# Adjacency products cut into quarter rows and spread anew over the turns of a two-step graph kernel

## The chip, the core and the metric

The program runs on one core of a Trainium2 chip. The metric is device time in microseconds (us); the median of three runs of the kernel before is 3864.36 us (3864.08 to 3867.04). TensorE (PE) multiplies matrices, VectorE (DVE), ScalarE (ACT) and GpSimd (POOL) work elementwise, and SyncE (SP) issues every DMA here. The engines run side by side, each in its own program order, and meet at semaphores.

## The reference

Two layers over 4096 nodes of 256 features. Layer 0 is graph attention with four heads. Layer 1 is run in two steps; in short:

```python
R = S + eye(N);  R = R / R.sum(-1)          # S is the 0/1 adjacency, 4096 x 4096
for n in range(2):
    A  = top_p_attention(Xa, W1, W2, W3)     # softmax(q @ k.T), kept up to 0.9 of the mass, 4096 x 4096
    Xf = R @ Xf
    Xa = A @ Xa
    Z  = Z + Xf @ U1[n].T + Xa @ U2[n].T
return layernorm(layernorm(X + Z) ... )      # the residual and norm around the layer
```

The change lies in the second of the two attention steps. There the kernel computes, beside the second A, both products with R (the two hops): R @ Xf and R @ (R @ Xf).

## The kernel before, in words

Rows are cut into 32 tiles of 128 nodes. The program is layer 0 (until about 1400 us), the first attention step (`s == 0`, until about 2180 us) and the second one (`s == 1`, to the end). In the second step a loop of *turns* n = 0, 1, 2, ... runs on every engine, with tiles staggered in it.

What TensorE does in turn n, in this order (lines 1056 to 1083): it transposes the finished probabilities of tile n-1 (`Tr`, L1029, 32 transposes), multiplies out the logits of tile n+2 (L984), does a small transpose (`zx`, L993), the product A @ Xa of tile n-1 (`AV`, L1044), a small product (`mq`, L1007), and then adjacency products: `Rmul` is one row tile of R @ Xf, 32 products with 257 columns (L967), whose four quarters use one 512 KB block of the adjacency each. Between two of these rows stands `gather_level` (L1050), one tiny product that brings 128 flags of tile n onto one partition.

A product in f32 is recorded as two MATMULs, so a row of 32 products is 64 records in the trace, and 32 in a listing of the program. There are 64 such rows: 0 to 31 are the first hop, 32 to 63 the second. `pairs_in(n)` says which pair of rows stands in turn n: rows 0 and 1 stand ahead of the turns, rows 2 and 3 in turn 0, rows 2n+2 and 2n+3 in every turn n up to 30.

What VectorE does for tile n: three passes of a threshold search over 128x4096 scores (L1577), one pass for the rest sum (L1583), maxima, a sort of 48 values, `threshold`, whose last instruction (L1637) releases `gather_level(n)` on TensorE. Then `finish(n)`: two marking passes (L1645, L1646), the read of TensorE's flags (L1691), the row maximum of tile n+2 (L1536), and the mask pass over tile n (L1710). The mask pass releases `Tr` of tile n, which is the first work of TensorE in turn n+1.

ScalarE copies results out of PSUM, runs the first three levels of the search for tile n+1 (`level`, L1314 and L1315), the exponentials (L1295), and copies out finished adjacency rows (`r_ev`, L1344). GpSimd computes the bracket for the search (`bracket`, L623 to L642; its L631 releases ScalarE's L1313) and finishes adjacency rows (`r_post`, L670 to L678). Finished rows go out through SP (`rstore`). Adjacency rows and AV share two PSUM banks in turn (`rslot`), and a bank is free once ScalarE has copied it out (`rv`).

SP loads adjacency blocks three ahead (`adjchunk`, a ring of AJR = 3 buffers): the block q+3 is asked for when TensorE is done with block q.

Of the kernel before, what the change touches and what calls it, by code (L numbers as in the profile page):

```python
# [9 lines left out]
ALU = mybir.AluOpType  # L10
# [16 lines left out]
def gat_topp_kernel(nc, xT, x, adj, adjTb, Wp, WT, aT, res_w, bias, res_b, ident, sel,  # L27
# [15 lines left out]
    AJR = 3  # L43
# [4 lines left out]
    RLEAD = 1  # L48
# [3 lines left out]
    fslot = {min(max(HT + m - RLEAD + 2, 2 * m + 4), NT + 1): m for m in range(HT)}  # L52
    LAST = max(fslot)
    DR = NT - 4

    def pairs_in(n):
        if n < 0:
            return [0]
        if n == 0:
            return list(range(1, RLEAD + 1))  # L60
        return [n + RLEAD] if n + RLEAD < NT else []

    ctx = ExitStack()
    with ctx:
# [273 lines left out]
        for s in range(2):  # L338
            g = {}
            names = ("kk", "pl", "el", "mx", "xp", "mask", "av", "rv", "pz", "po", "xs", "acc", "nz", "lv")  # L340
            if s == 0:
                names += ("kq", "ks", "gx", "gd", "lr", "xc")
            else:
                names += ("R", "rd", "hi", "gi", "yd", "ys", "fi", "fa", "s1", "f1", "s2", "fo", "fd", "lt", "e8", "bt",
                          "bf", "tp", "ls", "lp", "lz", "lo")
# [3 lines left out]
            g["xd"] = [sem(f"xd{i}_{s}") for i in range(2)]  # L349
            g["qd"] = [sem(f"qd{i}_{s}") for i in range(2)]  # L350
# [6 lines left out]
        def _(sp):  # L357
# [144 lines left out]
            def adjpairs(n, half):  # L502
                for p in pairs_in(n):
                    for q in range((2 * p + half) * NCH, (2 * p + half + 1) * NCH):
                        adjchunk(q + AJR)

            def rstore(n):
                for p in pairs_in(n):
                    for i in range(2):
                        r = 2 * p + i  # L510
                        sp.wait_ge(g["yd"], r + 1)
                        ld(tile_of(y_d if r < NT else z_d, r % NT), yr[:, i, :], g["ys"])
                    gxload(p + 1)
# [9 lines left out]
            adjpairs(-1, 1)  # L523
            for n in range(LAST + 4):
# [16 lines left out]
                if n in fslot:  # L541
# [10 lines left out]
                    sp.wait_ge(g["ys"], 16 * (NT + 2 * m + 2))  # L552
# [21 lines left out]
        def _(po):  # L574
# [36 lines left out]
            for s in range(2):  # L611
# [54 lines left out]
                def r_post(p):  # L666
                    for i in range(2):
                        r = 2 * p + i
                        po.wait_ge(g["rd"], r + 1)
# [1164 lines left out]
```

## Time and profile before

| | |
|---|---|
| median of three runs | 3864.36 us |
| the profiled execution's own time | 3867.65 us |
| span of its instructions on the core | 3865.9 us |
| mean granted TensorE clock | 0.983 |
| busy: PE, DVE, ACT, POOL | 94%, 92%, 79%, 39% |
| adjacency products (L967) in all | 909.5 us busy, 4096 records |

A timeline row reads: start in us, duration in us, engine, line, operation, out<-in, count; in square brackets, where the engine stood idle before it, how long and what ended the idle time. A row of windows reads: the stretch, its length, busy time (count) of each engine, the granted TensorE clock (1.00 is full speed), the DMA share and GB/s.

### The profile page before, as it was taken

The numbers are of one execution on the slowest core, as the hardware profiler recorded it, in microseconds if no ns is written. First come the engines' busy times: TensorE is split into PE (matmuls) and PEld (weight loads), VectorE is DVE, ScalarE is ACT, GpSimd is POOL, SyncE is SP. The second block draws the span as 40 slices with busy tenths as digits, with TensorE's granted clock in tenths as the row PEclk, the third lists the DMA queues.
The fourth block names the chain that finished last, engine by engine and source line by source line (L and its number), as shares of the span: only waits on it lengthen the run. The fifth ranks groups of instructions, "written<-read, shape, count | busy, mean of one in ns | idle before, by whom it ended". The sixth has DMA issues, their size and how long they took to land.

```text
span 3865.9 us, 66246 instructions
## 1 busy us (share of the span) xinstructions
PE 3617.3 (94%) x25368; PEld 3045.1 (79%) x25368; DVE 3559.9 (92%) x6051; ACT 3063.1 (79%) x3107; POOL 1522.2 (39%) x1627
## 2 busy tenths in 40 slices
PE   8888889889889879999999989999999999999997
PEld 5777778778778758777777768888888888888885
DVE  4999999999999989999999499999999999999998
ACT  6999999999999965555555378888888888888873
POOL 0112111111211210111111156555555569999997
PEclk9999999999999989999999989999999999999998
DMA  3211211211211140000000323333334433333332
GB/s 108 76 57 57 84 58 57 81 61 57 78 64 57 63 135 16 18 17 18 21 18 19 118 78 93 100 97 103 105 105 122 128 107 111 114 113 116 114 119 70
DMA packets 155582, 302.72 MB, mean 78 GB/s; under 512 B 16634, under 2 KB 116986, under 8 KB 151010
## 3 DMA queue, kind: packets, MB, share of 16 engines
q1 hardware_dynamic: 155234, 298.22, 24.2%
q8 instruction: 201, 3.29, 0.4%
q14 instruction: 147, 1.20, 0.1%
HBM read 256.54 MB, written 41.62 MB: 77 GB/s over the span
## 4 chain that ended last, share of the span: by engine, by line
ACT 35%; POOL 22%; DVE 21%; issue 12%; PE 10%; DVEq 0%; DMA 0%; ACTq 0%; SPq 0%; POOLq 0%
ACT b L1122 6%; ACT b L1314 6%; ACT b L1315 6%; ACT b L1135 5%; DVE b L1488 5%; ACT b L1115 4%; DVE b L1710 3%; POOL b L629 3%; POOL b L626 3%; DVE b L1470 3%; DVE b L1598 3%; DVE b L1596 2%; ACT b L1295 2%; POOL b L623 2%; PE ps L882 2%
## 5 line engine op out<-in xcount | busy, mean ns | idle before, releaser
L967 PE MATMUL ps<-b 128*128 128x257 f32 x4096 | 909.5, 382 | 6.2 <-DMA b<-in_adjTb 6.2
L1044 PE MATMUL ps<-b 128*128 128x257 f32 x4096 | 903.7, 380 | 0.0
L967 PEld LDWEIGHTS ps<-b 128*128 128x128 f32 x4096 | 776.4, 190 | 130.7 <-issue 9.7
L1044 PEld LDWEIGHTS ps<-b 128*128 128x128 f32 x4096 | 773.2, 190 | 112.9 <-ACT b L1252 0.8
L882 PE MATMUL ps<-cb,b 128*128 128x128 f32 x4096 | 517.6, 282 | 154.0 <-ACT b L1122 126.3
L882 PEld LDWEIGHTS ps<-cb,b 128*128 128x128 f32 x4096 | 462.3, 145 | 205.8 <-ACT b L1122 141.7
L1470 DVE SCALAR_TENSOR_TENSOR b<-b 128x4096 f32<-128x4096 f32 x128 | 566.5, 4425 | 13.6 <-ACT b L1115 9.3
L1472 DVE CUSTOM_DVE_ANT_0 b<-b 128x4096 f32<-128x4096 f32 x128 | 566.4, 4425 | 4.4
L589 POOL TENSOR_SCALAR b<-b 128x1 f32<-128x1 f32 x128 | 74.7, 584 | 1087.8 <-DVE b L1472 1087.8
L1135 ACT ACTIVATE b<-ps 128x1024 f32<-128x1024 f32 x510 | 487.1, 1051 | 18.2 <-PE ps L882 16.1
L822 PE MATMUL ps<-b 128*64 128x128 f32 x8192 | 488.9, 275 | 0.0
L1122 ACT ACTIVATE b<-b 128x4096 f32<-128x4096 f32 x127 | 476.1, 3749 | 15.6 <-POOL b L589 15.4
L822 PEld LDWEIGHTS ps<-b 128*64 128x64 f32 x8192 | 443.3, 137 | 26.8 <-ACT b L1135 10.9
L1577 DVE SCALAR_TENSOR_TENSOR b<-b 128x4096 f32<-128x4096 f32 x99 | 446.8, 4513 | 3.5
L1314 ACT ACTIVATE b<-b 128x4096 fp8e4<-128x4096 f32 x93 | 345.0, 3710 | 7.9 <-ACT b L1266 5.7
L1315 ACT ACTIVATE b<-b 128x4096 fp8e4<-128x4096 f32 x93 | 345.0, 3709 | 3.0
L1710 DVE SCALAR_TENSOR_TENSOR b<-b 128x4096 f32<-128x4096 f32 (+1 forms) x67 | 287.8, 4299 | 42.7 <-issue 27.4
L1115 ACT ACTIVATE b<-b 128x2560 f32<-128x2560 f32 x128 | 315.8, 2467 | 0.0
L1387 ACT ACTIVATE b<-ps 128x1024 f32<-128x1024 f32 x256 | 242.2, 1031 | 44.5 <-PE ps L1029 44.4
L1029 PE MATMUL ps<-cb,b 128*128 128x128 f32 x2048 | 242.1, 278 | 34.9 <-DVE b L1710 34.0
L1029 PEld LDWEIGHTS ps<-cb,b 128*128 128x128 f32 x2048 | 231.9, 144 | 45.2 <-DVE b L1710 40.6
L1295 ACT ACTIVATE b<-b 128x4096 f32<-128x4096 f32 x64 | 237.0, 3703 | 28.0 <-DVE b L1540 22.7
(212 smaller groups left out, 5038.6 us busy)
## 6 DMA issues: line engine op xcount, KB each, us to landing
b<-in_adjTb SPq DMA_DIRECT2D x256, 512.0 KB, 3.8
b<-in_adj SPq DMA_DIRECT2D x32, 2048.0 KB, 8.3
h_d<-b SPq DMA_DIRECT2D x63, 128.0 KB, 1.8
b<-h_d SPq DMA_DIRECT2D x63, 128.0 KB, 2.6
b<-in_xT SPq DMA_DIRECT2D x4, 1024.0 KB, 9.6
b<-in_xT SPq DMA_DIRECT2D x32, 128.0 KB, 8.1
X_d<-b SPq DMA_DIRECT2D x32, 128.0 KB, 8.3
gx_d<-b SPq DMA_DIRECT2D x32, 128.0 KB, 1.8
```

The lines of the kernel that those rows point to most:

```text
L822: last = mm(bank(6 + t % 2)[half, 128 * h:128 * h + 128], h_s[:, j, 64 * h:64 * h + 64], pt[:, gq % PTR, b, :], start=(j < 2), stop=(j >= ...
L882: last = nc.tensor.transpose(o[:, b * 128:(b + 1) * 128], ub[:, u % UB, j * 128:(j + 1) * 128], ident_s)
L967: last = mm(b[:, 0:XA], aj[:, q % AJR, e, :], xf[:, j, :], start=(j == 0), stop=(j == NT - 1))
L1029: last = nc.tensor.transpose(o[:, b * 128:(b + 1) * 128], scores(s, t)[:, j * 128:(j + 1) * 128], ident_s)
L1044: last = mm(o[:, 0:XA], at[:, q % ATR, b, :], xa[:, j, :], start=(j == 0), stop=(j == NT - 1))
L1115: act(ub[:, u % UB, LSP:N], sd_s[:, h, LSP:N], ACT.Identity, bias=ssc[:, t, h:h + 1]).then_inc(s_e, 1)
L1122: act(b, b, ACT.Exp, bias=nm[:, u % 4:u % 4 + 1], accum_out=zp[:, u % 16:u % 16 + 1]).then_inc(s_x, 1)
L1135: act(pt[:, gq % PTR].rearrange("p a b -> p (a b)"), bank(2 * (i % 3), 2)[:, 0:CW], ACT.Copy).then_inc(s_ev, 1)
L1314: alink(act(junk, e, ACT.Sign, bias=neg, accum_out=C, saturate=False))
L1315: alink(act(junk, e, ACT.Relu, bias=neg, accum_out=S, saturate=False))
L1470: link(v.scalar_tensor_tensor(out=b, in0=b, scalar=SLOPE, in1=b, op0=ALU.mult, op1=ALU.max))
L1472: v.tensor_tensor_reduce(out=b, in0=b, in1=adj_s[t % 2], scale=1.0, scalar=-3.0e38, op0=ALU.mult, op1=ALU.max, accum_out=nm[:, u % 4:u % 4 ...
```

## The change

The plan of adjacency rows is written in quarters (one 512 KB block each, 8 products, 16 records). Rows 0 and 1 still stand ahead of the turns. Turn 0 now holds rows 2, 3, 4 and 5 in place of 2 and 3, with the flags' product between the halves of row 4, and row 2 stands ahead of the logits of tile 2. Turns 1 and 2 hold two rows each, turns 3 to 10 seven quarters each instead of eight, and from turn 11 on all is as it was. Where a turn begins inside a row, the rest of that row (`head`) stands ahead of AV; the next whole row follows AV, then comes the flags' product, then what is left (`rest[1:]`). So after the flags' product there stand 3, 2, 1 and 0 quarters in turns 3, 4, 5 and 6, and 3, 2, 1 and 0 again in turns 7 to 10.

ScalarE copies out row 2 and 3 after the first and second level of turn 0 and a head row after the first level. GpSimd finishes four rows in its turn 0, and elsewhere the rows that ended in the turn before. The stores' semaphore is split in two by the parity of the row.

```diff
--- before.py
+++ after.py
@@ -45,20 +45,36 @@
     NQ = N // 512
     HT = NT // 2
     CT = 4
-    RLEAD = 1
     NGX = NT - 2
     KH = NT // 2
 
-    fslot = {min(max(HT + m - RLEAD + 2, 2 * m + 4), NT + 1): m for m in range(HT)}
+    fslot = {min(max(HT + m + 1, 2 * m + 4), NT + 1): m for m in range(HT)}
+    SHORT = range(3, 3 + 2 * NCH)
+
+    def row_plan():
+        plan = {0: ([], [(2, 0, NCH), (3, 0, NCH), (4, 0, NCH), (5, 0, NCH)])}
+        q = 6 * NCH
+        for n in range(1, NT - 1):
+            end = min(q + (2 * NCH - 1 if n in SHORT else 2 * NCH), 2 * NT * NCH)
+            head, rest = [], []
+            while q < end:
+                r, c = divmod(q, NCH)
+                hi = min(NCH, c + end - q)
+                (head if c else rest).append((r, c, hi))
+                q += hi - c
+            plan[n] = (head, rest)
+        assert q == 2 * NT * NCH
+        return plan
+
+    plan = row_plan()
+
+    def chunks_of(n):
+        return [r * NCH + c for part in plan.get(n, ((), ())) for r, lo, hi in part for c in range(lo, hi)]
+
+    def ended_in(n):
+        return [r for part in plan.get(n, ((), ())) for r, lo, hi in part if hi == NCH]
     LAST = max(fslot)
     DR = NT - 4
-
-    def pairs_in(n):
-        if n < 0:
-            return [0]
-        if n == 0:
-            return list(range(1, RLEAD + 1))
-        return [n + RLEAD] if n + RLEAD < NT else []
 
     ctx = ExitStack()
     with ctx:
...
@@ -549,24 +567,40 @@
                     if m >= 2:
                         sp.wait_ge(g["f1"], 2 * (m - 1))
                     sp.wait_ge(g["nz"], 16 * min(2 * m + 2, NT - 1))
-                    sp.wait_ge(g["ys"], 16 * (NT + 2 * m + 2))
+                    assert min(stored) >= HT + m + 1
+                    for i in range(2):
+                        sp.wait_ge(g["ys"][i], 16 * stored[i])
                     for i in range(2):
                         r = 2 * m + i
                         if r < NT - 1:
                             ld(fin[:, r % 6, :], tile_of(h_d, r), g["fi"])
                         ld(finz[:, i, :], tile_of(z_d, r), g["fi"])
                         ld(finx[:, r % 4, :], tile_of(X_d, r), g["fi"])
-                if HT in pairs_in(n):
-                    sp.wait_ge(g["ys"], 16 * (NT - 2))
+                if n == 0:
+                    adjrow(2)
+                    adjrow(3)
+                    rstore((0, 1))
+                    adjrow(4)
+                    rstore((2, 3))
+                    adjrow(5)
+                    continue
+                rows = (4, 5) if n == 1 else ended_in(n - 1)
+                todo = chunks_of(n)
+                if NT * NCH in todo:
+                    for i in range(2):
+                        sp.wait_ge(g["ys"][i], 16 * (HT - 1))
                     sp.wait_ge(g["R"], NT * NCH)
                     chunked(xf, y_d, 0, NQ - 1)
-                    rstore(n - 1)
-                    sp.wait_ge(g["ys"], 16 * NT)
+                    rstore(rows)
+                    for i in range(2):
+                        sp.wait_ge(g["ys"][i], 16 * HT)
                     chunked(xf, y_d, NQ - 1, NQ)
-                adjpairs(n, 0)
-                if HT not in pairs_in(n):
-                    rstore(n - 1)
-                adjpairs(n, 1)
+                for q in todo[:NCH]:
+                    adjchunk(q + AJR)
+                if NT * NCH not in todo:
+                    rstore(rows)
+                for q in todo[NCH:]:
+                    adjchunk(q + AJR)
             sp.wait_ge(g["fd"], 16 * NT)
             barrier(sp, kS[1])
 
...
@@ -663,20 +697,19 @@
                         po.wait_ge(g["hi"], 16 * (t + 1))
                     tt(hh, pzs, xa[:, t, 0:256] if s == 0 else hin, ALU.add).then_inc(g["acc"], 1)
 
-                def r_post(p):
-                    for i in range(2):
-                        r = 2 * p + i
-                        po.wait_ge(g["rd"], r + 1)
-                        plink(tt(prs[:, i, :], prs[:, i, :], xf[:, r % NT, :], ALU.add))
-                        plink(tt(pq[:, 1, i:i + 1], prs[:, i, 256:257], mone, ALU.pow))
-                        if p >= 1:
-                            po.wait_ge(g["ys"], 32 * p)
-                        o = ts(yr[:, i, :], prs[:, i, 0:256], pq[:, 1, i:i + 1], 0.0, ALU.mult, ALU.add)
-                        if r < NT:
-                            plink(o)
-                            po.wait_ge(g["gi"], 32 * (p + 1))
-                            o = tt(yr[:, i, :], yr[:, i, :], gxi[:, i, :], ALU.add)
-                        o.then_inc(g["yd"], 1)
+                def r_post(r):
+                    i = r % 2
+                    po.wait_ge(g["rd"], r + 1)
+                    plink(tt(prs[:, i, :], prs[:, i, :], xf[:, r % NT, :], ALU.add))
+                    plink(tt(pq[:, 1, i:i + 1], prs[:, i, 256:257], mone, ALU.pow))
+                    if r >= 2:
+                        po.wait_ge(g["ys"][i], 16 * (r // 2))
+                    o = ts(yr[:, i, :], prs[:, i, 0:256], pq[:, 1, i:i + 1], 0.0, ALU.mult, ALU.add)
+                    if r < NT:
+                        plink(o)
+                        po.wait_ge(g["gi"], 32 * (r // 2 + 1))
+                        o = tt(yr[:, i, :], yr[:, i, :], gxi[:, i, :], ALU.add)
+                    o.then_inc(g["yd"], 1)
 
                 def norm(r, dst, sem_):
                     a = lns[:, r % 4, :]
...
@@ -1062,10 +1096,15 @@
                         mq(n - 2, zx(n - 2, None))
                     if 1 <= n <= NT:
                         Tr(n - 1)
+                    if s == 1 and n == 0:
+                        Rmul(2)
                     if n + 1 + s < NT:
                         logits(n + 1 + s)
                     if n >= 2 and not early_z:
                         a = zx(n - 2, tx)
+                    head, rest = plan.get(n, ((), ())) if s == 1 else ((), ())
+                    for r, lo, hi in head:
+                        Rpart(r, part_of[r], lo * TBK, hi * TBK)
                     if 1 <= n <= NT:
                         AV(n - 1)
                     if n >= 2 and not early_z:
@@ -1073,13 +1112,22 @@
                     if tx is not None:
                         gx(tx)
                     if s == 1:
-                        for p in pairs_in(n):
-                            Rmul(2 * p)
-                            if n >= 1:
+                        if n == 0:
+                            Rmul(3)
+                            b4 = Rstart(4)
+                            Rpart(4, b4, 0, NT // 2)
+                            gather_level(n)
+                            Rpart(4, b4, NT // 2, NT)
+                            Rmul(5)
+                        else:
+                            for r, lo, hi in rest[:1]:
+                                part_of[r] = Rstart(r)
+                                Rpart(r, part_of[r], lo * TBK, hi * TBK)
+                            if n < NT:
                                 gather_level(n)
-                            Rmul(2 * p + 1)
-                        if n == 0 or n == NT - 1:
-                            gather_level(n)
+                            for r, lo, hi in rest[1:]:
+                                part_of[r] = Rstart(r)
+                                Rpart(r, part_of[r], lo * TBK, hi * TBK)
                 barrier(pe, kS[s])
 
         @block.scalar
@@ -1350,6 +1398,11 @@
                     for k in range(1, ACT_LEVELS + 1):
                         if t < NT:
                             level(t, k)
+                        if n == 0 and k <= 2:
+                            r_ev(k + 1)
+                        if n >= 1 and k == 1:
+                            for r, lo, hi in plan.get(n, ((), ()))[0]:
+                                r_ev(r)
                         if k == 2:
                             if 1 <= n <= NT:
                                 av_ev(n - 1)
@@ -1358,11 +1411,12 @@
                     if n < NT:
                         lc[0] += 1
                         ac.sem_inc(g["el"], 1)
-                    for r in items[:1]:
-                        r_ev(r)
+                    if n >= 1:
+                        for r in items[:1]:
+                            r_ev(r)
                     if n + 2 < NT:
                         expo(n + 2)
-                    for r in items[1:]:
+                    for r in items[1 if n >= 1 else 0:]:
                         r_ev(r)
 
                 if s == 1:
@@ -1400,7 +1454,8 @@
                         if tx is not None:
                             gx_ev(tx)
                     else:
-                        acts(n + 1, [2 * p + i for p in pairs_in(n) for i in range(2)], n)
+                        acts(n + 1, (4, 5) if n == 0 else
+                             [r for r, lo, hi in plan.get(n, ((), ()))[1] if hi == NCH], n)
                 barrier(ac, kS[s])
 
         @block.vector
```

TensorE's order, from the logits of tile 1 (L984 before, L1017 after) to the transposes of tile 0 (L1029, L1063). Adjacency products are L967 and L1000, the flags' product L1050 and L1084. Before:

```order
L984 MATMUL ps<-b 128x512 x8
L967 MATMUL ps<-b 128x257 x32
L984 MATMUL ps<-b 128x512 x8
L967 MATMUL ps<-b 128x257 x64
L1050 MATMUL ps<-cb,b 1x128
L1029 MATMUL ps<-cb,b 128x128 x32
```

After:

```order
L1017 MATMUL ps<-b 128x512 x8
L1000 MATMUL ps<-b 128x257 x64
L1017 MATMUL ps<-b 128x512 x8
L1000 MATMUL ps<-b 128x257 x48
L1084 MATMUL ps<-cb,b 1x128
L1000 MATMUL ps<-b 128x257 x48
L1063 MATMUL ps<-cb,b 128x128 x32
```

Rows 1 and 2 now follow each other (x64), the logits of tile 2 come one row later, and between them and the transposes stand three rows in place of two, with a row and a half of them behind the flags' product.

TensorE again, turn 6 of the loop: from the transposes of tile 5 to those of tile 6 (L1044 and L1078 are AV). Before:

```order
L1029 MATMUL ps<-cb,b 128x128 x32
L984 MATMUL ps<-b 128x512 x8
L993 MATMUL ps<-cb,b 128x128 x2
L1044 MATMUL ps<-b 128x257 x32
L1007 MATMUL ps<-b 128x256 x2
L967 MATMUL ps<-b 128x257 x32
L1050 MATMUL ps<-cb,b 1x128
L967 MATMUL ps<-b 128x257 x32
L1029 MATMUL ps<-cb,b 128x128 x32
```

After:

```order
L1063 MATMUL ps<-cb,b 128x128 x32
L1017 MATMUL ps<-b 128x512 x8
L1026 MATMUL ps<-cb,b 128x128 x2
L1000 MATMUL ps<-b 128x257 x24
L1078 MATMUL ps<-b 128x257 x32
L1040 MATMUL ps<-b 128x256 x2
L1000 MATMUL ps<-b 128x257 x32
L1084 MATMUL ps<-cb,b 1x128
L1063 MATMUL ps<-cb,b 128x128 x32
```

The 32 adjacency products that stood between the flags' product and the next transposes are gone from there; 24 of them (three quarters) stand ahead of AV, eight have gone to turn 0.

SP's queue in turn 0, from the load of tile 3's queries (kq_d) on. Before:

```order
L359 DMA b<-kq_d 64x128 [waits xp_1]
L359 DMA b<-kq_d 64x128
L359 DMA b<-in_adjTb 128x1024 [waits R_1] x4
L359 DMA y_d<-b 128x256 [waits yd_1] x2
L359 DMA b<-gx_d 128x256 x2
L359 DMA b<-in_adjTb 128x1024 [waits R_1] x4
L359 DMA b<-kq_d 64x128 [waits xp_1]
L359 DMA b<-kq_d 64x128
```

After:

```order
L376 DMA b<-kq_d 64x128 [waits xp_1]
L376 DMA b<-kq_d 64x128
L376 DMA b<-in_adjTb 128x1024 [waits R_1] x8
L376 DMA y_d<-b 128x256 [waits yd_1] x2
L376 DMA b<-gx_d 128x256 x2
L376 DMA b<-in_adjTb 128x1024 [waits R_1] x4
L376 DMA y_d<-b 128x256 [waits yd_1] x2
L376 DMA b<-gx_d 128x256 x2
L376 DMA b<-in_adjTb 128x1024 [waits R_1] x4
L376 DMA b<-kq_d 64x128 [waits xp_1]
L376 DMA b<-kq_d 64x128
```

Eight blocks are asked for ahead of the stores of rows 0 and 1 (y_d) in place of four, and the stores of rows 2 and 3 have come into turn 0.

## Rows read from the trace of the kernel before

**Rows 1.** Windows: turns 3 and 10.
```profile
2379.10:2429.70 50.60, 50.60 (x249) 42.25 (x248) 47.05 (x83) 41.83 (x47) 29.42 (x30) 1.00 0.33 100
...
2733.30:2784.00 50.70, 50.70 (x250) 42.30 (x249) 47.34 (x83) 41.83 (x47) 29.70 (x30) 1.00 0.33 101
```
**Rows 2.** Timeline of PE: turn 4, and the first row of turn 5.
```profile
2429.70 3.66 PE L1029 MATMUL ps<-cb,b 128*128 128x128 f32 x32
2433.29 3.71 PE L984 MATMUL ps<-b 64*128 64x512 f32 x16
...
2437.20 14.08 PE L1044 MATMUL ps<-b 128*128 128x257 f32 x64
...
2451.98 14.07 PE L967 MATMUL ps<-b 128*128 128x257 f32 x64
2465.98 0.38 PE L1050 MATMUL ps<-cb,b 128*1 128x128 f32 x2
2466.29 14.18 PE L967 MATMUL ps<-b 128*128 128x257 f32 x64
2480.31 3.66 PE L1029 MATMUL ps<-cb,b 128*128 128x128 f32 x32
```
**Rows 3.** Timeline of PE: from row 1 to the transposes of tile 0.
```profile
2217.12 2.85 PE L984 MATMUL ps<-b 64*128 64x512 f32 x12
2225.10 2.08 PE L984 MATMUL ps<-b 64*128 64x512 f32 x4 [5.13 <-ACT b L1252]
2227.11 26.38 PE L967 MATMUL ps<-b 128*128 128x257 f32 x112
2259.15 6.54 PE L967 MATMUL ps<-b 128*128 128x257 f32 x16 [5.66 <-DMA b<-in_adjTb]
2265.62 0.38 PE L1050 MATMUL ps<-cb,b 128*1 128x128 f32 x2
2276.00 6.59 PE L1029 MATMUL ps<-cb,b 128*128 128x128 f32 x32 [10.00 <-DVE b L1710]
2282.51 3.70 PE L984 MATMUL ps<-b 64*128 64x512 f32 x16
```
**Rows 4.** Timeline of DVE: the flags' read and the mask pass of tile 0.
```profile
2266.11 0.28 DVE L1691 TENSOR_REDUCE b<-ps 1x1 int32<-1x128 f32 x1 [4.27 <-PE ps L1050]
2266.42 4.43 DVE L1536 MAX8 b<-b 128x8 f32<-128x4096 f32 x1
...
2271.46 4.49 DVE L1710 SCALAR_TENSOR_TENSOR b<-b 128x4096 f32<-128x4096 f32 x1 [0.42 <-issue]
```
**Rows 5.** Waits, turns 2 to 11: engine line <- releaser: us, times, longest.
```profile
DVE b L1691 <- PE ps L1050: 21.2, 10, 2.4
```
**Rows 6.** Timeline of ACT: first level of turn 0, third level of turn 3 (ends).
```profile
2238.70 0.20 ACT L1313 ACTIVATE b<-b 128x1 f32<-128x1 f32 x1 [10.45 <-POOL b L631]
...
2248.10 0.29 ACT L1323 ACTIVATE b<-b 128x1 f32<-128x1 f32 x1
...
2420.70 0.29 ACT L1323 ACTIVATE b<-b 128x1 f32<-128x1 f32 x1
```
**Rows 7.** Timeline of POOL: row 0 finished.
```profile
2249.54 0.73 POOL L678 TENSOR_TENSOR b<-b 128x256 f32<-128x256 f32 x1
```
**Rows 8.** Timeline of PE: waits of 2.6 us in layer 0.
```profile
324.29 2.84 PE L882 MATMUL ps<-cb,b 128*128 128x128 f32 x24 [2.62 <-ACT b L1122]
...
365.84 5.38 PE L882 MATMUL ps<-cb,b 128*128 128x128 f32 x32 [2.62 <-ACT b L1122]
```
**Rows 9.** Windows: after waits of 2.62, 5.66 and 10.00 us.
```profile
365.84:371.20 5.36, 5.36 (x34) 5.36 (x34) 5.33 (x4) 5.36 (x5) 0.30 (x1) 0.68 0.00 0
...
2259.15:2265.60 6.45, 6.45 (x16) 4.92 (x16) 2.69 (x3) 6.38 (x5) 0.00 (x0) 0.56 0.26 102
2276.00:2282.50 6.50, 6.50 (x32) 6.35 (x32) 6.32 (x7) 3.45 (x4) 6.22 (x6) 0.54 0.04 10
2282.50:2286.00 3.50, 3.50 (x17) 1.47 (x16) 3.46 (x3) 3.33 (x4) 3.50 (x1) 1.00 0.02 5
```

More of the change, by code:

```diff
@@ L343, in gat_topp_kernel @@
             else:
-                names += ("R", "rd", "hi", "gi", "yd", "ys", "fi", "fa", "s1", "f1", "s2", "fo", "fd", "lt", "e8", "bt",
+                names += ("R", "rd", "hi", "gi", "yd", "fi", "fa", "s1", "f1", "s2", "fo", "fd", "lt", "e8", "bt",
                           "bf", "tp", "ls", "lp", "lz", "lo")
@@ L349, in gat_topp_kernel @@
             g["xd"] = [sem(f"xd{i}_{s}") for i in range(2)]
+            g["ys"] = [sem(f"ys{i}_{s}") for i in range(2)]
             g["qd"] = [sem(f"qd{i}_{s}") for i in range(2)]
@@ L500, in gxload, with adjrow, rstore @@
                         ld(gxi[:, i, :], tile_of(gx_d, 2 * p + i), g["gi"])
-            def adjpairs(n, half):
-                for p in pairs_in(n):
[L504 to L508, printed above, removed]
-                    for i in range(2):
-                        r = 2 * p + i
-                        sp.wait_ge(g["yd"], r + 1)
-                        ld(tile_of(y_d if r < NT else z_d, r % NT), yr[:, i, :], g["ys"])
-                    gxload(p + 1)
+            def adjrow(r):
+                for q in range(r * NCH, (r + 1) * NCH):
+                    adjchunk(q + AJR)
+            stored = [0, 0]
+            def rstore(rows):
+                for r in rows:
+                    sp.wait_ge(g["yd"], r + 1)
+                    ld(tile_of(y_d if r < NT else z_d, r % NT), yr[:, r % 2, :], g["ys"][r % 2])
+                    stored[r % 2] += 1
+                    if r % 2:
+                        gxload(r // 2 + 1)
             for c in range(NCH):
@@ L522, in _ @@
             qload(1, 2)
-            adjpairs(-1, 1)
+            adjrow(1)
             for n in range(LAST + 4):
@@ L664, in accumulate @@
                     tt(hh, pzs, xa[:, t, 0:256] if s == 0 else hin, ALU.add).then_inc(g["acc"], 1)
-                def r_post(p):
-                    for i in range(2):
-                        r = 2 * p + i
-                        po.wait_ge(g["rd"], r + 1)
-                        plink(tt(prs[:, i, :], prs[:, i, :], xf[:, r % NT, :], ALU.add))
-                        plink(tt(pq[:, 1, i:i + 1], prs[:, i, 256:257], mone, ALU.pow))
-                        if p >= 1:
-                            po.wait_ge(g["ys"], 32 * p)
-                        o = ts(yr[:, i, :], prs[:, i, 0:256], pq[:, 1, i:i + 1], 0.0, ALU.mult, ALU.add)
-                        if r < NT:
-                            plink(o)
-                            po.wait_ge(g["gi"], 32 * (p + 1))
-                            o = tt(yr[:, i, :], yr[:, i, :], gxi[:, i, :], ALU.add)
-                        o.then_inc(g["yd"], 1)
+                def r_post(r):
[11 more added lines that the diff above has]
+                    o.then_inc(g["yd"], 1)
                 def norm(r, dst, sem_):
@@ L718, in _ @@
                     if s == 1:
-                        for p in pairs_in(n - 1):
-                            r_post(p)
+                        for r in (0, 1, 2, 3) if n == 0 else (4, 5) if n == 1 else ended_in(n - 1):
+                            r_post(r)
                         if n - 2 in fslot:
@@ L1018, in _ @@
                 tat = {}
+                part_of = {}
                 def Tr(t):
```

2 lines of the change are left out of this document (1 added, 1 removed).

## The prediction, written before the changed kernel was timed

> **What bounds the kernel now.** I read the windows first, one for each turn that the change shortens. The reader is to see that a turn takes 50.6 us, that PE is busy in all of it and that its clock is granted in full [rows 1]; DVE is busy for 47 us of it, ACT for 42. The timeline of PE then shows the turn's parts without a gap: transposes, logits, AV, one adjacency row, the flags' product, a second row, and at once the next transposes [rows 2]. So in turns 3 to 10 the matmuls set the pace, and a quarter taken out of a turn (14.07 / 4 = 3.52 us) is worth 3.5 us, as long as no other wait ends last.
>
> The other wait is a loop through two engines. The mask pass of tile n releases the next transposes; it stands behind DVE's read of the flags, and that behind PE's own flags' product. Turn 0 shows its length with nothing behind the flags' product: PE finishes it at 2266.00 and then stands idle for 10.00 us until the mask pass is through [rows 3]. DVE uses these 10 us for the read, a row maximum of 4.43 us that stands between, and the mask pass of 4.49 us [rows 4]. None of it depends on the adjacency rows. In turn 4 of before, as in its neighbours, 14.02 us of adjacency work stand behind the flags' product and cover these 10 us with 4.0 to spare [rows 2].
>
> DVE's own loop, mask pass to mask pass, is 50.6 us less its mean wait for the flags of 21.2 / 10 = 2.1 us, so 48.5 us [rows 5]. No turn can be shorter than that for long, whatever PE has to do.
>
> **Turns 3 to 10, part by part.** Eight quarters leave: 8 x 3.51 = 28.1 us of PE work. Against it stands where the others now are. Turn 4 of before takes 2466.29 - 2429.70 = 36.6 us up to the end of the flags' product [rows 2]; each head quarter puts 3.5 us ahead of it and takes 3.5 us from behind it. With r quarters behind it PE waits for the mask for 10.0 - 3.5 r us, where that is above zero:
>
> Turn 3 has three behind, 10.5 us, and no wait: 47.1 us. Turn 4 has two, 7.0 us, a wait of 3.0: 50.1 us. Turn 5 has one, a wait of 6.5: 53.6 us. Turn 6 has none, a wait of 10.0: 57.1 us. Turns 7 to 10 repeat it. The waits are 2 x (3.0 + 6.5 + 10.0) = 39.0 us against the 28.1 us removed. The shift of quarters to the front of the turn costs more than their number brings.
>
> **The clock after the waits.** In turn 0 the 32 transposes behind the 10.00 us of idleness take 6.51 us (2276.00 to 2282.51) where they take 3.59 in turn 4 [rows 2, 3]; the 16 records behind 5.66 us of idleness take 6.47 instead of 3.52 [rows 2, 3]. The granted clock in these stretches is 0.54 and 0.56, and 1.00 right behind: PE ran near 1.2 GHz instead of 2.4 [rows 9]. So a wait of that size costs another 2.9 us in what follows, and all that follows (the flags' product too) is late by it. I charge it to the waits of 6.5 and 10.0 in turns 5, 6, 9 and 10: 4 x 2.9 = 11.6 us, the last of it paid in turn 11. For the waits of 3.0 us in turns 4 and 8 the nearest rows are waits of 2.62 us, of which one is followed by transposes at 5.38 us for 32 (3.66 is normal, so 1.7 lost, clock 0.68) and another by 24 at the full 2.84 us [rows 8, 9]. Bounds 0 and 1.7 each; I take 0, since PE had been busy without a break for some 47 us before these waits, which is more than in layer 0, and keep 3.4 us for the range.
>
> The Trainium skill has a rule that speaks against this change (TensorE: Matmul & The Clock Gate, "HAM oscillation — how this bites in real kernels"): a loop that makes PE wait in every iteration throttles it every time, and the loss is the throttled time x (1 - 1.2/2.4). The trace agrees for one such wait: about 6.5 us at the lower clock lost 2.9. By that rule the sum would hold 4 x 3.25 = 13 us in place of 11.6.
>
> Turn 7 begins on the lowered clock: its flags' product ends at 36.6 + 2.9 = 39.5, the 10.5 us behind it cover the mask, and it lasts 50.1 us, above DVE's 48.5. So DVE's floor adds nothing there. It would add 48.5 - 47.1 = 1.4 us if the clock stayed up.
>
> Sum for turns 3 to 11: -28.1 + 39.0 + 11.6 = +22.5 us.
>
> **Turn 0.** From 2217.12, the end of row 1, to 2282.51, the end of the transposes, before needs 65.4 us, of which 5.13 are a wait for ACT, 5.66 for an adjacency block and 10.00 for the mask, and the transposes run at the low clock [rows 3]. After, PE has four rows (4 x 14.05 = 56.2), logits 3.7, flags 0.3 and transposes 3.6: 63.8 us. One wait I expect: row 4 needs the bank of row 2, which ACT now copies out behind the first search level. That level ran from 2238.70 to 2248.4 [rows 6] and still can: the logits of tile 2 are through by about 2236, before GpSimd's bracket releases it. The copy also needs row 0 finished by GpSimd, at 2250.27 [rows 7]. So row 4 starts near 2250.9 where PE is ready at 2249.3: 1.6 us. With it 65.4 us, no change. DVE reads the flags without its 4.27 us of wait [rows 4] (they are on PE near 2258, DVE is ready at 2261.84), so the first mask comes 4.3 us earlier, and nothing uses it: PE is busy with row 5 until about 2279. Of the moved DMA issues, the block loads now run ahead of the first stores, so the stall of 5.66 us should go; the stores of rows 2 and 3 stand before row 5's last block, and that has some 7 us left. Bounds: -1.6 (no wait for the bank) to +8.6, should an adjacency block still come 5.66 us late and cost the clock again (2.95). I take 0.
>
> **What costs nothing.** ACT's copy of a head row (0.39 us) stands behind its first level, with 4.7 us between the end of turn 3's third level (2420.99) and the mask pass after which the search goes on from it (2425.7, turn 4's transposes of 2429.70 less the slack of 4.0) [rows 2, 6]. In turns 5, 6, 9 and 10 it may wait about 2 us for GpSimd; these are the long turns. Where a turn ends two rows of which the second begins a pair, its finishing on GpSimd waits until SP, which has the four block loads ahead of it, has stored the first: about 40 us into turns 5, 6 and 7. Behind it on GpSimd stand the scaling of AV's result and the next bracket, and the first is wanted by PE only in the next turn. Its cover is the rest of the turn; gone, it would cost a few us per turn. From turn 11 on nothing differs, so nothing is won back.
>
> **Rivals.**
> (a) *The turns shrink with their quarters.* The matmuls stay the bound, waits are filled. For it: PE has no idle time in these turns [rows 1]. Against it: the 10.00 us of [rows 3], with nothing in the program left to fill them. It could give at most the way down to DVE's 48.5 us, 8 x 2.1 = 17 us less: about 3847. It decides for faster only if the mask pass comes less than 47.1 - 40.1 = 7 us after the flags in turn 4, and less than 3.5 in turn 5. 4%.
> (b) *The waits come but the clock stays up.* Then -28.1 + 39.0 + 1.4 = +12.3: about 3877. For it: the 2.62 us that cost nothing [rows 8]. Against: both waits above 5.5 us in this step that the rows show cost 2.9 [rows 3, 9]. 12%.
> (c) *More is lost*: the short waits throttle too (+3.4) and turn 0 keeps its stall (+8.6): +34.5, about 3899. 11%.
> (d) *Hardly any change*: the mask follows the flags sooner in the late turns than in turn 0, say in 6 us, so that the waits are 2 x (2.5 + 6) = 17 us, the clock costs 4 x 2.9 or less, and -28.1 + 17 + 11.6 is near 0. Against: the read, the row maximum and the mask pass of [rows 4] are the same instructions in every turn. 4%.
> (e) My forecast, 69%.
>
> **The numbers.** The profiled execution took 3867.65 us (span 3865.9, 1.75 around it), 3.3 us above the median of the runs. 3867.65 + 22.5 = 3890.2 for such an execution, and 3864.4 + 22.5 = 3886.9 for the median: I predict 3887. The range is from 3874 (rival b with the -1.6) to 3899 (rival c). 0.2% of the time is 7.7 us, about what a measurement of this kernel tells from no change. Faster by more holds rival (a), 4%; within it rival (d) and a corner of (b), 5%; slower the rest, 91%.
>
> **What would show it.** On PE, in turns 3 to 6, idle time ended by the mask pass of about 0, 3, 6.5 and 10 us, and again in turns 7 to 10; transposes of 6.5 us and a granted clock near 0.55 behind the longer ones; turns of 47.1, 50.1, 53.6, 60.0, 50.1, 50.1, 53.6, 60.0 and 53.5 us for turns 3 to 11; the mask of tile 0 near 2271.7 and its transposes near 2279. The prediction is wrong if PE stays busy through turn 6, if the flags' product there stands idle in front of a ready DVE, or if the difference arises outside turns 0 to 11.

## The result, and the profile after

The changed kernel takes 3892.11 us (median of four runs, 3891.19 to 3895.25) against 3864.22 us of before in the same session: ratio 1.0072, 95% interval 1.006 to 1.0083, or 27.9 us slower. It was forecast at 3887 us.

The spans differ by 3893.4 - 3865.9 = 27.5 us. The timeline of PE in the changed kernel (columns as before; L1063 are the transposes that open a turn, turns 1 to 12 from top to bottom) shows where:

```profile
2280.22 3.66 PE L1063 MATMUL ps<-cb,b 128*128 128x128 f32 x32
...
2329.79 3.65 PE L1063 MATMUL ps<-cb,b 128*128 128x128 f32 x32
...
2380.39 3.66 PE L1063 MATMUL ps<-cb,b 128*128 128x128 f32 x32
...
2427.52 3.65 PE L1063 MATMUL ps<-cb,b 128*128 128x128 f32 x32
...
2477.30 5.38 PE L1063 MATMUL ps<-cb,b 128*128 128x128 f32 x32 [2.50 <-DVE b L1765]
...
2532.29 5.72 PE L1063 MATMUL ps<-cb,b 128*128 128x128 f32 x32 [5.97 <-DVE b L1765]
...
2591.09 5.34 PE L1063 MATMUL ps<-cb,b 128*128 128x128 f32 x32 [9.65 <-DVE b L1765]
...
2639.91 2.78 PE L1063 MATMUL ps<-cb,b 128*128 128x128 f32 x24
2643.79 1.09 PE L1063 MATMUL ps<-cb,b 128*128 128x128 f32 x8 [1.09 <-ACT b L1441]
...
2697.99 3.71 PE L1063 MATMUL ps<-cb,b 128*128 128x128 f32 x32 [2.82 <-DVE b L1765]
...
2751.62 5.29 PE L1063 MATMUL ps<-cb,b 128*128 128x128 f32 x32 [6.29 <-DVE b L1765]
...
2810.02 5.11 PE L1063 MATMUL ps<-cb,b 128*128 128x128 f32 x32 [9.67 <-DVE b L1765]
...
2862.08 3.65 PE L1063 MATMUL ps<-cb,b 128*128 128x128 f32 x32
```

The differences of the starts are the turns. Forecast and measured, in us:

| turn | 3 | 4 | 5 | 6 | 7 | 8 | 9 | 10 | 11 | sum |
|---|---|---|---|---|---|---|---|---|---|---|
| before | 50.6 | 50.6 | 50.6 | 50.6 | 50.6 | 50.6 | 50.6 | 50.6 | 50.6 | 455.5 |
| forecast | 47.1 | 50.1 | 53.6 | 60.0 | 50.1 | 50.1 | 53.6 | 60.0 | 53.5 | 478.1 |
| measured | 47.1 | 49.8 | 55.0 | 58.8 | 48.8 | 58.1 | 53.6 | 58.4 | 52.1 | 481.7 |

Behind turn 11 nothing differs: 1031.3 us from the start of turn 12 to the end of the span in both. The start of turn 3 comes 1.3 us later than before (2380.39 and 2379.10). Of that, 1.1 us lie ahead of PE's first adjacency record, where a block of logits took 5.40 us in this execution and 3.70 before. The windows of turns 3, 6 and 8 answer to [rows 1]: PE is busy in all of turn 3, but for 49.2 of 58.8 us in turn 6 and 50.6 of 58.1 us in turn 8, and in these two the granted clock is not full.

```profile
2380.39:2427.52 47.13, 47.13 (x234) 39.17 (x232) 43.77 (x83) 41.53 (x46) 26.60 (x29) 1.00 0.31 97
...
2532.29:2591.09 58.80, 49.16 (x232) 41.18 (x232) 46.61 (x83) 42.08 (x48) 30.16 (x29) 0.91 0.25 78
...
2639.91:2697.99 58.08, 50.60 (x234) 40.70 (x232) 46.80 (x81) 44.29 (x53) 28.63 (x28) 0.94 0.28 86
```

DVE's timeline of turn 6 answers to [rows 4]. It stood ready for 10.73 us in front of the late flags, and then took the same path as in turn 0: read, row maximum, mask pass, through at 2591.03, 0.06 us before the transposes.

```profile
2581.55 0.28 DVE L1746 TENSOR_REDUCE b<-ps 1x1 int32<-1x128 f32 x1 [10.73 <-PE ps L1084]
2581.87 4.43 DVE L1591 MAX8 b<-b 128x8 f32<-128x4096 f32 x1
...
2586.55 4.48 DVE L1765 SCALAR_TENSOR_TENSOR b<-b 128x4096 f32<-128x4096 f32 x1
```

Turn 8 is 8.0 us longer than forecast. Views of the changed kernel, read backwards. PE waits in front of the first adjacency row behind AV (row 19), for the PSUM bank of the head row 18, and runs row 19 on a lowered clock (granted 0.83 over the row; 16.93 us for 64 records, 14.07 in full):

```profile
2670.77 16.93 PE L1000 MATMUL ps<-b 128*128 128x257 f32 x64 [3.57 <-ACTq L1394]
```

ACT copies row 18 out behind its first level, but had waited 10.07 us for the bracket to begin that level:

```profile
2660.50 0.20 ACT L1361 ACTIVATE b<-b 128x1 f32<-128x1 f32 x1 [10.07 <-POOL b L665]
...
2670.22 0.39 ACT L1392 ACTIVATE b<-ps 128x257 f32<-128x257 f32 x1
```

And GpSimd had waited 13.72 us in turn 7 for the load of gx, the tile that it adds to a first-hop row to finish it, here row 16. SP issues it behind four block loads, the last of which waits for PE. The scaling of AV's result (L683, L688) then fell beside DVE's mask pass and its first search pass. Its two operations took 4.65 and 4.60 us and ended 0.4 us behind these passes; in turn 6, beside none, they took 0.57 and 0.48. So the bracket (from L657 on) began only at 2645.38, 5.5 us into turn 8, where that of turn 7 began 0.3 us into its turn. GpSimd:

```profile
2634.23 0.73 POOL L711 TENSOR_TENSOR b<-b 128x256 f32<-128x256 f32 x1 [13.72 <-DMA b<-gx_d]
...
2635.25 4.65 POOL L683 TENSOR_TENSOR b<-b,cb 128x1 f32<-128x1 f32 x1
2640.00 4.60 POOL L688 TENSOR_SCALAR b<-b 128x256 f32<-128x256 f32 x1
...
2645.38 0.24 POOL L657 TENSOR_SCALAR b<-b 128x1 f32<-128x1 f32 x1
```

DVE's passes at that time:

```profile
2634.99 4.49 DVE L1765 SCALAR_TENSOR_TENSOR b<-b 128x4096 f32<-128x4096 f32 x1 [0.39 <-issue]
...
2639.76 4.49 DVE L1632 SCALAR_TENSOR_TENSOR b<-b 128x4096 f32<-128x4096 f32 x1
```

### The profile page after: what moved, and what is told of

It is laid out like the page before. It is cut to its first block, busy times and chain, and to the rows that moved or that the text cites. A ratio compares the mean times of both kernels' runs of the same rounds, so it can differ in the third digit from the quotient of the medians.

```text
span 3893.4 us, 66261 instructions
## 1 busy us (share of the span) xinstructions
PE 3620.0 (93%) x25368; PEld 3043.1 (78%) x25368; DVE 3559.7 (91%) x6051; ACT 3063.5 (79%) x3107; POOL 1525.1 (39%) x1627
## 4 chain that ended last, share of the span: by engine, by line
ACT 26%; DVE 21%; PE 21%; POOL 18%; issue 11%; DVEq 0%; DMA 0%; ACTq 0%; SPq 0%; POOLq 0%
PE ps L1000 6%; ACT b L1170 6%; ACT b L1183 6%; PE ps L1078 5%; DVE b L1543 5%; ACT b L1163 4%; DVE b L1765 4%; ACT b L1362 3%; ACT b L1363 3%; DVE b L1653 3%; DVE b L1525 3%; DVE b L1651 2%; PE ps L915 2%; PE ps L1063 2%; POOL b L663 2%
## 5 line engine op out<-in xcount | busy, mean ns | idle before, releaser
L1000 PE MATMUL ps<-b 128*128 128x257 f32 x4096 | 908.7, 381 | 5.9 <-ACTq L1394 5.1
L1078 PE MATMUL ps<-b 128*128 128x257 f32 x4096 | 902.7, 380 | 0.0
L1000 PEld LDWEIGHTS ps<-b 128*128 128x128 f32 x4096 | 773.6, 190 | 130.2 <-issue 8.8
L1078 PEld LDWEIGHTS ps<-b 128*128 128x128 f32 x4096 | 771.9, 190 | 114.0 <-ACT b L1300 0.8
L1183 ACT ACTIVATE b<-ps 128x1024 f32<-128x1024 f32 x510 | 486.9, 1052 | 17.2 <-PE ps L915 15.2
L1063 PE MATMUL ps<-cb,b 128*128 128x128 f32 x2048 | 247.3, 281 | 63.9 <-DVE b L1765 61.6
L1063 PEld LDWEIGHTS ps<-cb,b 128*128 128x128 f32 x2048 | 235.9, 146 | 76.5 <-DVE b L1765 71.4
L1343 ACT ACTIVATE b<-b 128x4096 f32<-128x4096 f32 x64 | 237.0, 3703 | 39.2 <-DVE b L1595 34.7
```

The source lines that it names most:

```text
L1000: last = mm(b[:, 0:XA], aj[:, q % AJR, e, :], xf[:, j, :], start=(j == 0), stop=(j == NT - 1))
L1063: last = nc.tensor.transpose(o[:, b * 128:(b + 1) * 128], scores(s, t)[:, j * 128:(j + 1) * 128], ident_s)
L1078: last = mm(o[:, 0:XA], at[:, q % ATR, b, :], xa[:, j, :], start=(j == 0), stop=(j == NT - 1))
L1183: act(pt[:, gq % PTR].rearrange("p a b -> p (a b)"), bank(2 * (i % 3), 2)[:, 0:CW], ACT.Copy).then_inc(s_ev, 1)
```

## The experiments

Every ratio is against the kernel before, run on the same chip in the same session. The sessions differ between some of the runs; the medians of before in them lie between 3864.22 and 3865.58 us.

**e3: the place alone.** In the kernel before, the flags' product of turns 3 to 10 is moved two quarters back.

```diff
                             Rmul(2 * p)
+                            if 3 <= n <= 10:
+                                b2 = Rstart(2 * p + 1)
+                                Rpart(2 * p + 1, b2, 0, NT // 2)
+                                gather_level(n)
+                                Rpart(2 * p + 1, b2, NT // 2, NT)
+                                continue
                             if n >= 1:
```

Expected: 

> The kernel before with one thing moved: in turns 3 to 10 the flags' product stands in the middle of the second adjacency row, with two quarters (7.0 us) behind it in place of four. No quarter changes its turn and no row is split over turns. Theory 1: PE waits 3.0 us (2.5 to 3.0 by the changed kernel) for the mask in each of the eight turns, 20 to 24 us, and where the clock falls up to 1.8 us more per turn: 3884 to 3902 us. Theory 2 (split rows): no change, 3864 us.

Measured 3897.97 us against 3864.64, ratio 1.0083 (1.0067 to 1.01), as theory 1 has it. No quarter changed its turn, no row was split, and 33 us are lost: the eight waits are 20.9 us, and the transposes behind them lost 13.2 us. PE's timeline, transposes that open turns 4 to 6, shows the wait and, from the second on, the clock's price:

```profile
2426.38 3.71 PE L1029 MATMUL ps<-cb,b 128*128 128x128 f32 x32 [2.51 <-DVE b L1716]
...
2479.70 5.38 PE L1029 MATMUL ps<-cb,b 128*128 128x128 f32 x32 [2.50 <-DVE b L1716]
...
2534.69 5.38 PE L1029 MATMUL ps<-cb,b 128*128 128x128 f32 x32 [2.49 <-DVE b L1716]
```

**e1: the place put right.** In the changed kernel the flags' product follows the fourth quarter of every turn, with three behind it.

```diff
-                            for r, lo, hi in rest[:1]:
...
+                            seq = [(r, c) for r, lo, hi in rest for c in range(lo, hi)]
+                            first = NCH - sum(hi - lo for r, lo, hi in head)
+                            for i, (r, c) in enumerate(seq):
+                                if i == first and n < NT:
+                                    gather_level(n)
```

Expected: 

> The changed kernel with the flags' product of turns 3 to 10 moved: always right behind the fourth adjacency quarter of the turn (head quarters counted), so that three quarters (10.5 us) stand behind it in each; the number of quarters per turn stays seven. Theory 1 (the place of the flags' product causes the loss, since its mask follows 10.0 us later): the waits of 2.5 to 9.7 us in front of the transposes go, turns 3 to 10 run at DVE's own loop of about 48.5 us, and the sum over turns 3 to 11 falls from 481.7 to about 438 us: about 3848 us in all. With some turns at 50 us where ACT or GpSimd come last, up to 3860. Theory 2 (the loss comes from rows split over two turns: banks, copies behind a search level, stores): hardly changed, 3885 to 3892.

Measured 3874.67 us, ratio 1.0025 (1.0016 to 1.0035), between the two theories. The waits for the mask are gone, and with them 17 us of the loss; but the 44 us that theory 1 asked for did not come. PE now waits elsewhere, inside the transposes, whose last eight need a PSUM bank that ACT has not copied out. The waits of turns 3 to 11 (engine line <- releaser: us, times, longest):

```profile
ACT b L1363 <- POOL b L665: 53.9, 9, 10.4
POOL b L711 <- DMA b<-gx_d: 47.7, 3, 18.0
...
PE ps L1063 <- ACT b L1443: 18.1, 7, 5.5
```

**e4: gx row by row.** In the changed kernel GpSimd's gx is loaded as soon as the row two before is stored.

```diff
-            def gxload(p):
-                if p < HT:
-                    for i in range(2):
-                        ld(gxi[:, i, :], tile_of(gx_d, 2 * p + i), g["gi"])
+            def gxload(r):
+                if r < NT:
+                    ld(gxi[:, r % 2, :], tile_of(gx_d, r), g["gi"][r % 2])
...
-                    if r % 2:
-                        gxload(r // 2 + 1)
+                    gxload(r + 2)
```

Expected: 

> The changed kernel with the loads that GpSimd needs to finish first-hop rows (gx) issued row by row as soon as the row two before is stored, on a semaphore for each parity, in place of pair by pair. Theory 1: turn 8's extra 8 us (ACT waits 10.1 us for GpSimd's bracket, PE 3.6 us for the bank of row 18, and the clock falls) come from GpSimd's waits of 13.7 to 14.2 us for gx in turns 5, 6 and 7, above all in turn 7, which delay the scaling and then the bracket; without them turn 8 takes about 50 us: 3884 us. Theory 2 (turn 8 is late because the short turn 7 leaves ACT and GpSimd no time anyway): GpSimd's waits go, but turn 8 stays near 58 us: 3892 us.

Measured 3886.28 us, ratio 1.0053 (1.0037 to 1.007). Turn 8 lasts 2685.24 - 2634.20 = 51.0 us in place of 58.1, by PE's timeline:

```profile
2634.20 2.78 PE L1063 MATMUL ps<-cb,b 128*128 128x128 f32 x24
...
2685.24 5.14 PE L1063 MATMUL ps<-cb,b 128*128 128x128 f32 x32 [2.81 <-DVE b L1765]
```

The bracket of that turn now begins 2.3 us into it. So turn 8's extra time came from the wait for gx. The medians differ by 5.8 us, and turns 3 to 11 of the profiled executions by only 3.6 (481.7 and 478.1): behind the same waits the transposes lost more in this run (6.58, 5.78 and 6.59 us in place of 5.72, 5.34 and 5.29).

**e8: PE kept busy.** e4, with products that nobody reads in the place of the idle time (the expectation says how many).

```diff
+                            for _ in range({4: 6, 5: 13, 6: 21, 8: 6, 9: 13, 10: 21}.get(n, 0)):
+                                mm(bank(2 * ((lc[0] - 1) % 3) + 1)[:, 0:256], ident_s, xf[:, 0, 0:256],
+                                   start=True, stop=True)
```

Expected: 

> The changed kernel with gx loaded row by row, and with products that nobody reads put behind the flags' product in turns 4, 5, 6, 8, 9 and 10 (6, 13 and 21 of 256 columns, of about 0.43 us each), so that TensorE works through the time it otherwise waits for the mask. The run without them took 3886.3 us and its transposes behind the waits took 4.05, 6.58, 5.78, 5.14, 6.59 and 5.78 us for 3.65. Theory 1 (part of the loss is the lowered clock, which follows from idleness and not from the wait as such): these transposes take 3.65 us, 12.0 us in all are gained, 3874.3 us. Rival (the transposes are slow for another reason, the waits being there as before): 3886 us.

Measured 3879.09 us, ratio 1.004 (1.0026 to 1.0053). Putting in 80 products made it 7.2 us faster than e4, which ran in another session (before is 3864.28 us in this one and 3864.64 in that). The five runs lie between 3877.98 and 3881.26 us, the four of e4 between 3885.69 and 3887.01. The transposes that open turns 6 and 7 take full speed again (granted 1.00, and 0.55 and 0.63 in e4), and the mask still comes as late:

```profile
2529.12 3.71 PE L1063 MATMUL ps<-cb,b 128*128 128x128 f32 x32 [0.36 <-DVE b L1768]
2585.91 3.71 PE L1063 MATMUL ps<-cb,b 128*128 128x128 f32 x32 [0.39 <-DVE b L1768]
```

Turns 3 to 11 fell from 478.1 to 468.9 us, 9.2 of the expected 12.0. What is missing is mostly turn 7, which now reaches DVE's loop: 48.7 us, with waits of 1.35 us for DVE and 1.17 us for ACT. So the lowered clock follows from PE's idleness, and costs 7 to 9 us in this version.

**e2: turn 0 alone.** Eight quarters in each of turns 1 to 29.

```diff
-    SHORT = range(3, 3 + 2 * NCH)
+    SHORT = ()
```

Expected: 

> The changed kernel with eight quarters in every turn from 1 to 29 and none in turn 30: turn 0's four rows alone, no split rows, the eight quarters saved at the end. Theory 1 (turn 0 costs nothing): turn 1's transposes at about 2280 us end as in the changed kernel, turns 3 to 11 take 50.6 us each, and turn 30, 46.8 us of which were matmuls, ends with its mask some 6 us earlier at best, of which the lowered clock takes 2 to 3 back: 3858 to 3865 us. Theory 2 (a share of the loss is in turn 0's rows, stores and copies): above 3870 us.

Measured 3864.76 us, ratio 1.0001 (0.9991 to 1.001), as theory 1 has it. Turn 0's rows cost nothing, and neither do the split semaphore of the stores and the copies behind the search levels of turn 0, which this version has too. The eight quarters saved at the end also bring nothing; why was not looked at.

**e5: e1 and e4 together.** Expected: 

> Both edits together: the flags' product behind the fourth quarter of each turn, and gx loaded row by row. In the run with the first edit alone the waits for the mask are gone, but turns 5, 7, 8, 10 and 11 took 51.6, 57.1, 53.6, 52.1 and 57.5 us, with ACT waiting up to 10.4 us for GpSimd's bracket. Theory A (the bracket is late because GpSimd waits for gx in turns 5 to 7): turns 7 and 8 come down to about 50 us, and the whole to about 3862 us. Theory B (the loop from ACT's levels over the exponential and the bracket back to the levels is the floor, since the bracket's operations pass only between DVE's passes, so that a turn shorter than 50.6 us makes the next one longer): it stays above 3870 us.

Measured 3863.04 us, ratio 0.9995 (0.9986 to 1.0005): theory A's number, though not by its turns. Turn 8 came down to 48.3 us, but turn 7 still took 53.7 where 50 were expected, and turns 10 and 11 together 107.6. The version is back at the time of before, not below it.

**e6: the short turns spread.** Expected: 

> As the run before, but the eight turns of seven quarters are 3, 4, 6, 7, 9, 10, 12 and 13 instead of 3 to 10, so that DVE's loop of 48.5 us is hardly undercut. Theory A: turns 3 to 14 take 48.5 us on average, 25 us less than before, near 3842 us. Theory B (ACT and GpSimd have a loop of about 50.6 us, of which a split row's copy makes 51.2): turns of 50.6 to 51.5 us, 3865 to 3875 us.

```diff
-    SHORT = range(3, 3 + 2 * NCH)
+    SHORT = (3, 4, 6, 7, 9, 10, 12, 13)
```

Measured 3864.55 us, ratio 0.9997 (0.9988 to 1.0007). Theory A's 3842 fell; theory B's lower bound is 3865.

**e7: three copy buffers.** e6 with `prs` 3 deep, and r_ev(r) waiting for row r-3 in place of r-2. To make room, seven small tiles (`fac`, `avg`, `onesr`, `am`, `iota`, `w8`, `lns`) lie elsewhere in the core's memory. Expected: 

> As the run before, with three buffers in place of two for adjacency rows copied out by ACT, so that the copy of a head row does not wait for GpSimd (about 1.9 us in turns 5, 6, 9 and 10 of the changed kernel). Theory A (these waits push the bracket past a gap between DVE's passes): up to 10 us less than the run before. Theory B (the copies' own length and the loop of 50.6 us do it): within 3 us of the run before.

Measured 3862.26 us, ratio 0.9994 (0.9984 to 1.0004). At 2.3 us less than e6 this is within theory B's bound, and within what the runs scatter: the copies' wait for GpSimd was not the main thing.

**e9: one row moved, four short turns.** Turn 0 holds rows 2, 3 and 4; otherwise as e7.

```diff
-    SHORT = (3, 4, 6, 7, 9, 10, 12, 13)
+    SHORT = (3, 6, 9, 12)
...
-        plan = {0: ([], [(2, 0, NCH), (3, 0, NCH), (4, 0, NCH), (5, 0, NCH)])}
-        q = 6 * NCH
+        plan = {0: ([], [(2, 0, NCH), (3, 0, NCH), (4, 0, NCH)])}
+        q = 5 * NCH
```

Expected: 

> One row in place of two moved to turn 0 (rows 2, 3 and 4 there), four short turns (3, 6, 9 and 12) in place of eight, flags' product always behind the fourth quarter, gx by row, three copy buffers. Turn 0: the mask of tile 0 comes 4.3 us earlier than in the kernel before and now is what PE waits for (about 6.7 us of idleness, lowered clock behind it as before), so turn 1 starts 4.3 us earlier. Short turns: 4 x 3.5 = 14.1 us, if a short turn that stands alone meets neither DVE's loop nor the wait for ACT in the transposes. Theory A (the second floor, ACT's copies behind the exponential, binds only where short turns follow each other): about 18 us less than before, 3846 to 3852 us. Theory B (it binds at every short turn or after it, as the third turn of each group in the runs before): 3858 to 3865 us.

Measured 3856.26 us, ratio 0.998 (0.9971 to 0.9989): between the theories, though nearer to B. Turns 3 to 8 came to the tenth of a microsecond as A has them; the late ones did not. ACT's timeline of turns 9 and 10 shows what the earlier runs had hidden. Its copy of the turn's first whole row stands ahead of the exponential, and where head quarters come first (two in turn 9, three in turn 10), that row ends late on PE, so the exponential (L1343), and the bracket after it, wait for PE:

```profile
2713.14 0.39 ACT L1392 ACTIVATE b<-ps 128x257 f32<-128x257 f32 x1 [1.37 <-PE ps L999]
2713.72 3.71 ACT L1343 ACTIVATE b<-b 128x4096 f32<-128x4096 f32 x1 [0.19 <-ACT b L1392]
...
2764.53 0.39 ACT L1392 ACTIVATE b<-ps 128x257 f32<-128x257 f32 x1 [2.12 <-PE ps L999]
```

**e10: the copy behind the exponential.** e9 with one edit:

```diff
-                    if n >= 1:
-                        for r in items[:1]:
-                            r_ev(r)
+                    k = 0 if n == 0 or plan.get(n, ((), ()))[0] else 1
+                    for r in items[:k]:
+                        r_ev(r)
...
-                    for r in items[1 if n >= 1 else 0:]:
+                    for r in items[k:]:
```

Expected: 

> The last run (one row moved, four short turns; 3856.3 us) with ACT's copy of the turn's first whole row behind the exponential in turns that begin inside a row. In that run turns 3 to 8 came as reckoned (47.1 and 50.6 us), but in turns 9 to 11 ACT stood 1.4 to 2.1 us in front of that copy, waiting for PE, so that exponential, bracket and levels fell behind, and turns 10, 11 and 13 took 51.4, 51.4 and 56.7 us. Theory A (this copy is what breaks the late turns): turns 9 to 14 take 47.1 or 50.6 us each, 8.7 us less: 3848 us. Theory B (any further short turn runs into DVE's and ACT's loops): within 3 us of 3856.

Measured 3847.73 us (five runs, 3845.35 to 3849.65) against 3864.78, ratio 0.9957 (0.9943 to 0.9971), as theory A has it (3848). It is 17 us faster than before and 44 faster than the changed kernel. PE is busy without a gap from turn 3 to turn 14, by the window:

```profile
2371.00:2978.30 607.30, 607.30 (x2992) 504.76 (x2991) 575.58 (x997) 510.10 (x575) 350.88 (x354) 1.00 0.33 103
```

and turn 3 begins at 2372.32 and turn 15 at 2965.80: 593.5 us where 12 turns of before take 607.3, 13.8 less, nearly the 14.1 us of the four quarters. The other gain is in turn 0, whose mask pass now ends last there: turn 1 starts 87.5 us behind PE's first adjacency record (2182.85 to 2270.30), 91.3 before (2184.68 to 2276.00), and its transposes take 5.52 us in place of 6.59.

**e11: the same edit with two rows moved** (on e7). Expected: 

> The same edit of the copy on the version with two rows moved, eight short turns of 3 to 14 and three copy buffers (3862.3 us). Theory A: the short turns in pairs no longer leave ACT behind; turns 3 to 14 take 48.5 to 49 us on average where they took 50.1: 3843 to 3850 us. Theory B (two short turns in a row undercut DVE's and ACT's loops by 1.4 us each, and the bracket then misses a gap between DVE's passes, whatever the copy does): above 3855 us.

Measured 3853.14 us, ratio 0.9971 (0.9959 to 0.9982): 9 us better than e7 and between the theories: 3 us above theory A's range and 2 below theory B's bound. Behind each second short turn in a row PE still waits for ACT within the transposes (1.6 to 2.6 us), and behind three of the four for the mask as well (0.2 to 0.7 us). Turn 11 opens so:

```profile
2768.45 2.84 PE L1063 MATMUL ps<-cb,b 128*128 128x128 f32 x24 [0.16 <-DVE b L1767]
2773.64 1.15 PE L1063 MATMUL ps<-cb,b 128*128 128x128 f32 x8 [2.35 <-ACT b L1443]
```

So other loops than PE's, DVE's and ACT's, do bind there. How much of it is the bracket missing a gap between DVE's passes was not taken apart.

## Why the prediction was right, and where its sizes were off

**The place against the number of quarters: right.** The waits were reckoned at 3.0, 6.5 and 10.0 us twice, 39.0 in all; the trace has 2.50, 5.97, 9.65, 2.82, 6.29 and 9.67, 36.9 in all; by the turns' lengths up to 0.2 us more at the shorter ones (turn 4: 49.78 - 47.13 = 2.65). e3 shows the mechanism without the rest of the change, and e1 takes it away.

**The quarters removed: right.** Turn 3, with no wait, fell from 50.6 to 47.1 us.

**The clock: right in kind, a little large.** Reckoned at 4 x 2.9 = 11.6 us. Above the normal 3.65 us the transposes lost 2.1, 1.7, 1.6 and 1.5 us behind the four long waits, and 1.7 behind the 2.50 us of turn 4, for which I had taken 0: 8.6 in all. The granted clock over these transposes was 0.64 to 0.72, and not 0.55 as in the rows of turn 0. The short wait can cost as much as the long one, or nothing (2.82 us in turn 8), and the 47 us of unbroken work for which I took 0 did not protect the transposes behind turn 4. Another 2.9 us of clock lie in turn 8, in row 19, behind a wait that the sum did not have. The rule that the prediction cites from the Trainium skill (TensorE: Matmul & The Clock Gate, "HAM oscillation — how this bites in real kernels"), a loss of half of the throttled time, agrees with these transposes too: 5.38 us at a granted 0.68 are 5.38 x 0.32 = 1.7 us lost.

**Turn 0: right.** From PE's first adjacency record to the end of turn 0's transposes it took 2283.80 - 2185.75 = 98.1 us, and before 2282.51 - 2184.68 = 97.8. The wait for row 2's bank was 1.53 us (1.6 reckoned), the stall for an adjacency block went, and the mask came 4.2 us earlier measured from the same point, unused. e2 says the same in time.

**The step that was mis-sized: "what costs nothing".** It named the very chain, GpSimd's finishing of a row that waits until SP has its four block loads behind it, and said that its cover is the rest of the turn and that gone it would cost a few us. In turns 5 and 6 the cover held: when gx had landed, 11.7 and 15.2 us were left of turns of 55 and 59 us. In turn 7, of 49 us, 5.7 were left, the scaling behind the wait met DVE's passes, the bracket began 5.5 us into turn 8, and turn 8 cost 58.1 us instead of 50.1. The prediction took turns 5, 6 and 7 together and did not work out the cover of the shortest. That term, set at 0, measured 7 to 8 us (e4 took 7.0 of it away). It is the largest miss of the sum, and the total hides part of it: the eight other turns together came out 4.4 us under their forecast, so that turns 3 to 11 took 3.6 us more than forecast, and the medians differ by 27.9 where 22.5 were forecast. That the forecast came so near is luck to that extent. Rival (c), with +34.5, expected more loss from other causes, and its larger one, a stall in turn 0, did not come. A slip without effect: the lower end of the range, 3864.4 + 12.3 - 1.6, is 3875 and not 3874.

**DVE's loop of 48.5 us: right as a bound, not the only one.** In rival (a) and in e1's expectation I took it for the floor of a turn. e1, e6 and e11 show a second one beside it: bracket on GpSimd, levels, exponential, and the copies of the transposes on ACT. Its length was not measured: in the kernel before it is hidden, since all turns there take 50.6 us.

## What to carry to other kernels

In a software pipeline, ask of every product that another engine waits for how much work stands behind it before this engine needs the answer; moving work from behind it to before it costs the full length of that work, here 3.5 us per quarter, once the spare time (here 4.0 us) is used up, even when the total shrinks. Where a wait is said to be covered, weigh the cover in the shortest turn that the change makes. And when a change fails, look at what it was for: with the flags' product, one load and one copy in the right places, and with half as much moved (one row, four short turns that stand apart), the same idea gained 17 us.

## What the runs showed that I had not expected

80 products without any use made the kernel 7.2 us faster (3886.28 to 3879.09), by keeping TensorE's clock up through waits that they did not shorten.

Behind waits of 2.49 to 2.82 us the 32 transposes took between 3.71 and 6.67 us, and in one run (e3) a wait of 2.51 us in turn 3 cost nothing and one of 2.50 us in turn 4 cost 1.7 us. Single such terms scatter by up to 3 us between turns, so a forecast is safer for a sum over several of them than for one.
